# S6 scan of a fused network: the sum over states taken in pairs on GpSimd, one product of 512 columns a pair on TensorE

## The reference

```python
dt, Bm, Cm = jnp.split(u @ xproj_w.T, [DT_RANK, DT_RANK + DSTATE], axis=-1)
dt = jax.nn.softplus(dt @ dt_w.T + dt_b)
A = -jnp.exp(A_log)
def step(h, inp):
    dt_t, B_t, C_t, u_t = inp
    dA = jnp.exp(dt_t[..., None] * A)
    h = dA * h + (dt_t * u_t)[..., None] * B_t[:, None, :]
    y = jnp.einsum('bdn,bn->bd', h, C_t)
    return (h, y)
...
return ys.transpose(1, 0, 2) + u * D_p
```

## Time and profile before

| | us |
|---|---|
| median of 3 runs | 1645.13 |
| profiled execution, time | 1643.63 |
| profiled execution, span | 1641.8 |
| TensorE busy | 1499.9 |
| VectorE busy | 1259.8 |
| ScalarE busy | 1186.2 |
| GpSimd busy | 521.1 |

### The profile page before, as it was taken

One profiled execution on the slowest core, in us unless ns is written; L12 is line 12 of the kernel. 1 busy time (PEld: TensorE's weight loads), 2 busy tenths in 40 slices (PEclk: granted clock), 3 DMA queues, 4 the chain that ended last, 5 costly groups with the idle time before them and its releaser, 6 DMA issues.

```text
span 1641.8 us, 35130 instructions
## 1 busy us (share of the span) xinstructions
PE 1499.9 (91%) x14164; PEld 952.0 (58%) x14164; DVE 1259.8 (77%) x2393; ACT 1186.2 (72%) x2411; POOL 521.1 (32%) x414
## 2 busy tenths in 40 slices
PE   4899999798999999999999999988898999999997
PEld 2566665344456666666666666644444566666664
DVE  4898978866568868787688989787675787778874
ACT  4657486356898978778875776844668987787886
POOL 2643400000135535544234532000012354345530
PEclk9999999799999999999999999989999999999999
DMA  5422215430001011101132411355000011001011
GB/s 189 155 102 70 91 37 110 111 63 4 7 8 28 21 24 24 24 14 40 35 105 92 129 60 58 84 121 115 5 1 14 5 40 27 18 8 27 21 34 29
DMA packets 53585, 88.20 MB, mean 54 GB/s; under 512 B 5840, under 2 KB 27088, under 8 KB 51664
## 3 DMA queue, kind: packets, MB, share of 16 engines
q1 hardware_dynamic: 53424, 85.96, 19.7%
HBM read 55.65 MB, written 15.60 MB: 43 GB/s over the span
## 4 chain that ended last, share of the span: by engine, by line
PE 37%; DVE 33%; ACT 21%; issue 5%; DMA 2%; SPq 1%; POOL 1%; DVEq 0%; ACTq 0%; POOLq 0%
DVE neg_max L1252 8%; ACT tiles L1645 5%; PE psum L635 4%; DVE tiles L1173 4%; PE psum L729 3%; ACT tiles L1593 3%; PE psum L936 3%; PE psum L711 3%; ACT tiles L1687 2%; PE psum L904 2%; DVE ssq L1287 2%; DVE lsum L1304 2%; PE psum L1002 2%; DVE tiles L1427 2%; DVE tiles L1178 2%
## 5 line engine op out<-in xcount | busy, mean ns | idle before, releaser
L635 PE MATMUL psum<-cst,tiles 128*128 128x128 f32 x1440 | 211.1, 282 | 28.2 <-ACT tiles L1687 3.9
L1802 POOL TENSOR_TENSOR tiles<-cst,b_columns 128x512 f32<-128x512 f32 x128 | 159.0, 1259 | 220.1 <-PE psum L711 173.9
L635 PEld LDWEIGHTS psum<-cst,tiles 128*128 128x128 f32 x1440 | 159.9, 142 | 108.8 <-issue 48.5
L1252 DVE TENSOR_REDUCE neg_max<-psum 128x2 f32<-128x1024 f32 (+3 forms) x176 | 187.4, 1120 | 44.4 <-PE psum L856 44.3
L1813 POOL TENSOR_TENSOR tiles<-tiles 128x512 f32<-128x512 f32 x64 | 81.7, 1277 | 427.7 <-DVE tiles L1428 423.3
L1645 ACT ACTIVATE tiles<-psum,lmax,invn 128x128 f32<-128x128 f32 x512 | 191.1, 480 | 23.3 <-DVE lmax L1300 14.6
L1825 POOL TENSOR_TENSOR tiles<-tiles,lsum 128x1024 f32<-128x1024 f32 x64 | 121.3, 1898 | 206.0 <-DVE lsum L1306 205.9
L1173 DVE TENSOR_TENSOR_SCAN tiles<-tiles,psum 128x512 f32<-128x512 f32 x128 | 149.3, 1203 | 18.7 <-PE psum L711 16.4
L1542 ACT ACTIVATE tiles<-tiles,colp 128x512 f32<-128x512 f32 x128 | 89.4, 717 | 87.5 <-DVE tiles L1173 80.1
L1593 ACT ACTIVATE tiles<-psum 128x1024 f32<-128x1024 f32 (+1 forms) x128 | 113.8, 922 | 44.6 <-PE psum L856 33.0
L711 PEld LDWEIGHTS psum<-tiles 128*128 128x128 f32 x1024 | 124.8, 192 | 35.0 <-issue 22.7
(11 more groups left out here) (230 smaller groups left out, 3439.0 us busy)
## 6 DMA issues: line engine op xcount, KB each, us to landing
tiles<-bc_scratch SPq DMA_DIRECT2D x64, 512.0 KB, 3.8
v_prev<-tiles SPq DMA_DIRECT2D x112, 128.0 KB, 2.3
split_scratch<-tiles SPq DMA_DIRECT2D x96, 128.0 KB, 2.4
tiles<-split_scratch SPq DMA_DIRECT2D x32, 384.0 KB
wts<-in_wts SPq DMA_DIRECT2D x1, 3114.0 KB, 14.5
tiles<-in_x SPq DMA_DIRECT2D x8, 256.0 KB, 3.2
out<-tiles SPq DMA_DIRECT2D x8, 256.0 KB, 2.4
tiles<-in_tab SPq DMA_DIRECT2D x1, 768.0 KB, 8.6
```

What stands on the lines that cost most here:

```text
L635: ins = nc.tensor.transpose(ps[:, j * 128:(j + 1) * 128], src[:, j * 128:(j + 1) * 128], ident)
L1252: nc.vector.tensor_reduce(nm[:, j, :, i * n:(i + 1) * n], ps.rearrange("p (e n) -> p e n", e=2)[:, :, 0:n * keys].rearrange("p e (a n) -> ...
L1802: tt(blocks(T(S6_B[n % 2])), ident.unsqueeze(1).to_broadcast([P, NJ, 128]), own(b_columns)[:, :, n:n + 1].to_broadcast([P, NJ, 128]), ALU. ...
```

## The change

`y_sum` no longer reads the two tiles of a pair. A new unit `hc_pair(m)` on GpSimd waits for `hc(m)` and adds the second tile to the first in place; `y_sum(m)` waits for `hc_pair(m)` and takes one product of 512 columns with the first tile. The additions of a pair are thus made in f32 in SBUF, the eight pairs still in PSUM. The orders of all five engines and the banks are laid out anew: GpSimd's has 64 units more (394 for 330), the others have the units that they had, in another order.

```diff
-              (HC, "hc", m), ("PE", "y_sum", m)]
+              (HC, "hc", m), ("POOL", "hc_pair", m), ("PE", "y_sum", m)]
...
                 def y_sum(m):
                     prepared("fetched", "cst")
-                    pe.wait_ge(*at("hc", m))
+                    pe.wait_ge(*at("hc_pair", m))
                     if m == 0:
                         prepared("skip")
                         take("y_sum", 0, freed_by=[at("mx")])
                         mm(place("y_sum", 0), skip[:, :], T(XRT), start=True, stop=False)
-                    for a in range(2):
-                        ins = mm(place("y_sum", m), ident, T(S6_H[m % 2] + a), start=False, stop=(m == STATES // 2 - 1 and a == 1))
-                    full(ins)
+                    full(mm(place("y_sum", m), ident, T(S6_H[m % 2]), start=False, stop=(m == STATES // 2 - 1)))
...
+                def hc_pair(m):
+                    pool.wait_ge(*at("hc", m))
+                    tt(T(S6_H[m % 2]), T(S6_H[m % 2]), T(S6_H[m % 2] + 1), ALU.add).then_inc(sem("hc_pair"), 1)
```

More of the change, by code:

```diff
@@ L217 @@
[L217 to L220, removed]
@@ new lines @@
+    "POOL": (
+        "80180000000100300400600200700900500a00c00800d00f00b00g00i00j00l00m00e00h10110000k10300n10410610710210910a10510c10d20110f"
+        "10g10810b10i10j20010l10m10e10h10k20420320710n20620a20920d20c20220520g20f20j20i20m20l20820b20e20h30030120k30320n304306302"
+        "30730930a30c30530d00o30830f30g30b30i30j30m30l30e30h30k30n10o20o30o00p00q00s00t00r00u00v00w00y00z00x10p10q10s10t10r01010v"
+        "10w10u10y10z10x20p20q11020r01101230p20s20t30q01420u01520v20w30s30t01330r20x01601730u01830v30w20y20z11111221001a30y30z01b"
+        "11411530x01911301c31011611711821121211a21411b11921521311c21721621831131221a21b31431521931331621c31731831a31b31940040131c"
+        "40440340740240640a40940d40540c40g50050140840f40j40b40e40i40m40l40h50450340k50750650a50950d40n50250c50550g50f50j50i50850m"
+        "50b50l50e50h50k60060150n60460360760660a60260960d60560c60g60f60j60i60860m60l60b60e60h60k70070160n70370470670270770970a70c"
+        "70d70f70570870g70i40o70j70b70l70e70m70h70k70n50o60o70o40p40q40s40t40r40v40u40w50p50q40y40z40x50s50t41050r50u50v50w50y50z"
+        "50x51060p60q41141270p60s60t60r41441570q70s60u70t41360v60w70r60x70u41641741870v70w60y60z51151241a41b61070y70z51441951570x"
+        "51341c71051751851651a51b51951c71171271471561161271361461571661361671771861761871a71b71961a61b61971c61c"),
@@ new lines @@
+    "SP": (
+        "80480680880780110080080200080580320080980a80b300001002003004005006007301008302009201202101102103104105203106107108109204"
+        "20520620720820930330430530630700a30830900b00c10a10b10c00d00e10d20a10e20b20c30a30b30c20d20e00f00g30d30e00h00i10f10g10h20f"
+        "20g10i20h00j30f20i00k10j30g10k00l30h00m10l30i10m20j20k00n40030j20l20m30k10n50030l30m40140240350150220n600404405503406407"
+        "40840930n70050450550650750850960160260360460560670170260760870360970470570670770840a40b70940c50a50b50c40d40e60a60b60c50d"
+        "50e70a70b70c60d60e40f40g70d70e40h50f40i50g50h60f50i60g40j60h70f60i40k70g40l50j70h40m70i50k60j50l50m40n60k70j70k60l50n70l"
+        "60m70m70n60n"),
@@ new lines @@
+    "015315145135315315146170350203156232152671352450150630160626426071570251271423124720240762460202457024502340124247601254"
+    "201401267071026145167125043612315631256740203240203514073150710560203456745262040263206735134654346537260230201453241026"
+    "126756571201452460412356235235234010356745032031456040120120102132012345672415362161512136104526405705602402402302514035"
+    "627034013015064121274152147601325071012515712345416740230102314507207324254701234671340102103103102013024542014567014021"
@@ L367 @@
+    "015632021346715601565017467327316527250427315604602467043621050247270124574514576061201602307217260760507157602605267167"
+    "650463217071301012030240230245701203403454670453601304107102012012014012120102130102404213265173412131315340314230123501"
+    "021345062152524034020567425071070610342101021010200123456405102101")
 class Waiting:
@@ L1825, in l_probs @@
                     tt(pr, pr, own(lsum)[:, j % 2, :].unsqueeze(2).to_broadcast([P, LHEADS, 128]), ALU.mult).then_inc(sem("l_probs"), 1)
-                run("POOL", {"v_zero": v_zero, "b_diagonal": b_diagonal, "ve_ones": ve_ones, "k_rot": k_rot, "l_probs": l_probs, "qk_sum": qk_sum, "bias_split": bias_split})
+                run("POOL", {"v_zero": v_zero, "b_diagonal": b_diagonal, "hc_pair": hc_pair, "ve_ones": ve_ones, "k_rot": k_rot, "l_probs": l_probs, "qk_sum": qk_sum, "bias_split": bias_split})
             @block.sync
```

266 lines of the change are left out of this document (124 added, 142 removed).

## The result

The changed kernel takes 1676.05 us (median of 4 runs, 1672.75 to 1677.94) beside 1645.36 us of the kernel before on the same chip: ratio 1.0189, 95% interval 1.0174 to 1.0204. It is 31 us slower where I forecast 32 us faster, and it lies above the range of 1590 to 1650. The profiled execution took 1676.99 us, its span is 1675.2.

The account below looks back on a forecast made before the run. TensorE, 95.5% busy, was taken to bound S6, VectorE 23 us behind. Start -7, first stretch +9, between -18, second -10, behind -13, contention +5, late tiles +2: -32 from span 1641.8, time 1613; 8-in-10 range 1590 to 1650.

Parts of the forecast that it names:

- TensorE sets the pace there: S6 stretches: TensorE, busy 336.1 of 352 us (95.5%), bounds them, with VectorE at 88.9%, 23 us behind.
- the 7 for contention and late tiles: S6 stretches: +5 us for contention and +2 us for scans waiting on the longer chain of a pair.
- the orders' saving outside S6: Outside the S6 stretches: less work in the new orders, -7 us ahead, -18 between, -13 behind.
- The cost of the products, 55 us: `y_sum` in S6: 64 f32 products of 512 columns removed at 0.86 us each, TensorE from 1500 to 1445.
- The addition, 1.26 us: `hc_pair` on GpSimd: 64 f32 additions of 128x512 at 1.26 us each, 81 us in all.
- Hidden on GpSimd: S6 stretches: GpSimd's load goes from 150 to 230 of some 350 us, hidden if its queue is well ordered.
- Contention, +5: S6: GpSimd additions delay `hc` and other two-input VectorE operations on SBUF, 8 us today becoming 12; bounds 0 and 56.
- Rival 3: S6: contention undoes the gain, every pair's `hc` meeting a GpSimd operation, 56 us; +21, 1666 us; chance 0.16.
- its sign for contention: Profile after, S6: `hc` at a mean over 1.8 us, or `hc_pair` near 2, would show contention.
- The longer chain, +2: S6: `y_sum` waits for `hc_pair`, `hc` to free tiles 2.1 or 3.2 us instead of 1.72; 2 us charged.
- The new orders by stretch: S6: VectorE's 163 and 172 us of work at 95.5% give 171 (+9) and 180 (-10); between -18, behind -13.
- The start, -7: Ahead of S6: VectorE has 7 us less to do before the first scan (33 to 26), TensorE 13; -7 us.

Follow-up runs that it names:

- the 128 fillers: Kernel before with 128 bf16 products of 512 columns (constants) more on TensorE, one ahead of each `dbu`'s waits in S6: 1642.83 us, 0.9995.
- the short addition: Changed kernel with `hc_pair` adding 8 of 512 columns, all waits kept, the rest of the odd states left out: 1662.28 us, 1.0102.
- the addition put aside: Changed kernel with GpSimd adding constants into another tile, same length and places, `y_sum` waiting for `hc` alone, odd states left out: 1673.71 us, 1.0179.

## Why the prediction was wrong, point by point

- **"TensorE sets the pace there": failed, and with it the sign.** I read 95.5% busy as the engine that bounds, against VectorE's 88.9%. In the old orders, taking one product of each pair away with nothing added gave +8.5 us; adding 128 gave -0.5. VectorE's work, with the chain that it stands in, counted nearly one for one when added, and 16 of 36 us when taken away. The Trainium skill (Perfetto Trace Analysis, Identifying the Most-Contended Engine) says that matmul busy time tells little of TensorE's headroom, and weight loads more; the rows agree, for PEld was busy 67% and 65% in the earlier trace rows, and the 128 fillers fitted in. I had the note on modelled ends before me and still compared the two shares as if alike. The table of waits was no help either: I read VectorE's 16.4 us of waits for `dbu` as TensorE being late; with TensorE's 64 products gone VectorE's idle time in S6 stayed (17.6 + 23.8 us for 17.3 + 21.9).
- **Where the 65 us between forecast and result lie.** In the S6 stretches +38 came for +6 (with the 7 for contention and late tiles), 32 us of it. Outside them -5 came for -38, 33 us. So the orders' saving outside S6, which I had priced one for one, is half of the miss.
- **The cost of the products, 55 us: right in size** (TensorE's busy time for `y_sum` fell by 51.9), worth nothing in the old orders and 22 us in the new ones, which had first cost 42. The rest of TensorE's operations drew longer by 22, so its busy time fell by 30 only.
- **The addition, 1.26 us: right** (1.27 in the middle, 1.40 in the mean). **Hidden on GpSimd: wrong.** GpSimd had the room, and its queue held, but its reads didn't leave VectorE alone.
- **Contention, +5: wrong in size.** I priced it on `hc`, as both the term and its bound did. `hc` rose by 1.8 us. VectorE's busy time rose by 25.6, in operations that I hadn't put in the sum, and the two runs that differ in the addition's length alone differ by 22.5 of it (1262.9, 1285.4) and by 14 us of time. Rival 3 had the right sign and, at 1666, the nearest time, but named the wrong operation: its sign for contention, `hc` over 1.8 us, never came.
- **The longer chain, +2: right** in the new orders, where the short addition was free (1662 beside 1664). The scans stood 7.9 us for `y_sum`, but 9.7 without any addition, so the orders cause that wait and not the hop. In the old orders VectorE's added idle time was 21, from chain and queue together.
- **The new orders by stretch.** In S6 I divided VectorE's 163 and 172 us by 0.955: 351. Measured are 365.6 us of busy time and 390 us. 365.6 / 0.955 is 383, so most of the miss of 39 is busy time that I hadn't counted (31 us: contention, and what its neighbours in the windows add), and the rest its pace of 93.7%. Outside S6 TensorE's busy time fell by 31 us (1133 for 1164), for the 45 that I had counted. The time there fell by 5 only: 12 less ahead of S6, nothing between the stretches, 7 more behind. So behind the start TensorE's saving was worth nothing, and work added there cost little as well (6 us for 128 fillers in the heads, 3.4 in the windows).
- **The start, -7: right in kind**, -12.
- **What the orders do wrong is open in part.** They move 25 us of VectorE's work into S6 (335 for 310 by my count), where added work counted nearly one for one. With what was drawn out, VectorE's busy time in the stretches is 52.8 us more than in the earlier trace rows (365.6 for 312.8) and its idle time 15 us less; the difference is the 38 us of the stretches. Why VectorE's work taken out of the heads and windows gave nothing back, while work put in there costs 29 and 17 us, isn't shown: no run parts one engine's order from the others'. Open too is why one product fewer costs 8.5 us in the old orders; `hc` was drawn out by 6.1 us in that run, which may be how it now falls against `b_diagonal`.

## What to carry to other kernels

Don't rank TensorE against another engine by busy shares: put 128 idle products in and see whether the time moves, and do the same with the other engine, before work is taken from either. Put the filler where no other engine waits for it, or it measures the chain as well, and try it in the orders that the change will have: here the same saving was worth nothing in one set of orders and 22 us in another. Price work moved to GpSimd by what it does to every VectorE operation that reads two tiles in SBUF or copies from one in the stretch, not by its most frequent one. And a saving off the pace is lost, while orders laid out for it can carry work into the stage where it counts nearly in full.

## What the runs showed of the hardware

- A VectorE operation with one tile from SBUF and a scalar a partition (`k_cols`, 128x512) meets GpSimd as well: 516 ns at least, 1267 in the middle in the changed kernel, for 541 before. The Trainium skill (SBUF — State Buffer, Who interferes with whom) names this form among those that can take the shared port, and the trace agrees. With the short addition it is back at 548, and with the addition put aside at 1164, so that middle goes with the addition's length. `b_diagonal` alone can do it too: of the six slow ones in the changed kernel three overlap no addition but a `b_diagonal` (1039 to 1354 ns), and `q_cols`, the same operation, took 1266 ns beside one at 918.6 us before. The scan, with one input from PSUM, stays at 1221 ns at most beside 192 GpSimd operations of the stretches.
- Busy time of TensorE is elastic: fillers that take 28 us, by the distance to the next start, raised it by 11.6 us.
- Fillers raised the granted clock in S6 from 0.97 and 0.96 to 0.98 and 0.99 in the old orders with one product a pair, and the median time didn't fall (1654.2 us for 1652.6).
